# Two-layer network over 16 sequences: the last two blocks as a pair, first-pass steps moved between stages, and the second pass's upper queries in halves

## The reference

```python
# first layer ("first pass")
s = causal_attention(xn)        # 16 heads of 64, softmax over 256 keys, then Wo
g = silu(moe(xn))               # top-1 of 8 experts (352 wide) + a shared expert
# second layer
s = linear_attention(xn)        # 16 heads of 8, elu + 1, cumulative sums
g = silu(transformer(xn))       # two layers l = 0, 1 ("second pass")
# one layer of the transformer: shift tokens, q k v, l2norm, rotary with decay,
# 8 heads of 64, window of 64 tokens:
bk, bv = look_around(bk), look_around(bv)      # the block of 64 before, and its own
mask = (i < j) | (i > j + WINDOW) | (j == -1)  # WINDOW = 64
# then wo, layer norm, glu of width 341, and back to 128
```

## Time and profile before

| | |
|---|---|
| median of 3 runs | 2231.97 us |
| the profiled execution | 2232.22 us, its span 2230.4 us |
| PE busy | 1856.1 us, 83% |
| DVE busy | 1273.5 us, 57% |
| ACT busy | 1248.0 us, 56% |
| POOL busy | 785.9 us, 35% |
| mean granted TensorE clock | 0.914 of full speed |
| chain that ended last | PE 60%, DVE 15%, ACT 9%, issue 8%, POOL 6% |

### The profile page before, as it was taken

How to read it: one execution, slowest core, us unless ns; L and a number is a source line. 1 busy time by engine, 2 the same in 40 slices (tenths; PEclk the granted TensorE clock), 3 DMA queues, 4 the chain that set the end, 5 groups by cost and what they waited for, 6 DMA issues and landing times.

```text
span 2230.4 us, 34655 instructions
## 1 busy us (share of the span) xinstructions
PE 1856.1 (83%) x10900; PEld 1157.0 (52%) x10900; DVE 1273.5 (57%) x4083; ACT 1248.0 (56%) x3559; POOL 785.9 (35%) x912
## 2 busy tenths in 40 slices
PE   6689998997899888987899689987898789858766
PEld 4367764654455455554555345644555445535434
DVE  4434556546755467445754575546745575467654
ACT  2445546754765566656665575656664576346444
POOL 2732225323532343224431353324332343244431
PEclk9889999998999999988999799998999899979878
DMA  8155510000000000000000000000000000000000
GB/s 233 36 173 163 162 39 10 1 1 6 1 1 15 6 1 1 15 1 1 6 6 11 1 1 1 20 1 1 1 13 3 1 1 6 4 2 1 6 0 6
DMA packets 49711, 53.26 MB, mean 24 GB/s; under 512 B 6386, under 2 KB 42236, under 8 KB 49532
## 3 DMA queue, kind: packets, MB, share of 16 engines
q0 software_dynamic: 7808, 27.79, 3.8%
q1 hardware_dynamic: 41724, 23.26, 3.7%
HBM read 41.60 MB, written 9.44 MB: 23 GB/s over the span
## 4 chain that ended last, share of the span: by engine, by line
PE 60%; DVE 15%; ACT 9%; issue 8%; POOL 6%; DMA 1%; DVEq 0%; SPq 0%; POOLq 0%; ACTq 0%
PE ps L552 6%; PE ps L596 5%; PE ps L670 5%; PE ps L568 4%; PE ps L521 4%; PE ps L544 3%; PE ps L541 3%; PE ps L578 3%; PE ps L679 3%; ACT p L813 3%; DVE big L1162 2%; PE ps L512 2%; PE ps L531 2%; POOL h L293 2%; PE ps L725 2%
## 5 line engine op out<-in xcount | busy, mean ns | idle before, releaser
L975 DVE CUSTOM_DVE_ANT_0 p<-ps,mask,nrq 128x128 f32<-128x128 f32 (+1 forms) x512 | 183.0, 413 | 253.4 <-PE ps L544 253.4
L552 PE MATMUL ps<-ident,p 128*128 128x128 f32 x1536 | 250.4, 294 | 48.1 <-ACT p L813 47.3
L1272 POOL COPY rdx<-rden 128x256 f32<-128x256 f32 x256 | 94.7, 399 | 554.6 <-DVE rden L991 554.6
L975 DVE CUSTOM_DVE_ANT_0 p<-ps,mask 128x128 f32<-128x128 f32 (+1 forms) x512 | 152.3, 353 | 232.7 <-PE ps L544 218.1
L552 PEld LDWEIGHTS ps<-ident,p 128*128 128x128 f32 x1536 | 172.8, 147 | 156.6 <-issue 153.1
L813 ACT ACTIVATE p<-p,nmax 128x256 f32<-128x256 f32 x512 | 253.8, 496 | 0.0
L812 ACT ACTIVATE p<-p,nmax 128x128 f32<-128x128 f32 x512 | 200.4, 391 | 67.1 <-DVE nmax L975 66.8
L670 PE MATMUL ps<-wqkv,hT 128*128 128x512 f32 x384 | 208.1, 658 | 27.7 <-ACT big L890 27.3
L826 ACT ACTIVATE pt<-ps 128x384 f32<-128x384 f32 x256 | 125.7, 491 | 175.6 <-PE ps L552 175.6
L531 PE MATMUL ps<-ident,big 128*128 128x128 f32 x512 | 92.2, 325 | 124.7 <-DVE big L1167 94.4
L1377 POOL TENSOR_TENSOR big<-big,rots 128x512 f32<-128x512 f32 x64 | 87.9, 1374 | 274.7 <-ACT big L890 268.2
(11 more groups left out here) (214 smaller groups left out, 3977.6 us busy)
## 6 DMA issues: line engine op xcount, KB each, us to landing
slots_in<-xn SPq DMA_DIRECT2D x1, 2560.0 KB, 14.6
v<-slots_in SPq DMA_DIRECT2D x20, 128.0 KB, 4.7
slots_out<-v SPq DMA_DIRECT2D x20, 128.0 KB, 1.8
big<-in_x SPq DMA_DIRECT2D x4, 512.0 KB, 6.2
x<-in_x SPq DMA_DIRECT2D x8, 256.0 KB, 4.1
out_x<-x SPq DMA_DIRECT2D x8, 256.0 KB, 2.3
wqkv<-in_wqkv SPq DMA_DIRECT2D x2, 768.0 KB
xn<-in_x SPq DMA_DIRECT2D x6, 256.0 KB, 3.2
```

The source lines that it names most:

```text
L552: last = nc.tensor.transpose(bank[:, j * P:(j + 1) * P], c.p[:, u % 4, j * P:(j + 1) * P], c.ident[:, :])
L975: last = V.tensor_tensor_reduce(out=c.p[:, u % 4, a:b], in0=bank[:, a:b], in1=c.mask[st.kind][:, P * (1 - i):SEQ], scale=scale, scalar=3e3 ...
```

## The change

Four things are changed together.

1. **Order.** The prologue leaves ticks 16 to 21, amid the expert stages, without attention; `fill` of the 18 ticks now pauses only at 8, 9, 12 and 13, so that 14 of 18 hold attention (0 to 7, 10, 11, 14 to 17). Each of blocks 0 to 5 so takes 8 first-pass pairs and not 7, and the 64 pairs are used up before block 6. Blocks 6 and 7 then go as a pair: layer 0 of block 6, 2 empty ticks, layer 0 of block 7, 8 empty ticks, layer 1 of block 6, 2 empty ticks, layer 1 of block 7. The side stages go with their blocks. The list has 307 ticks.
2. **Buffers.** Block 7 has its linear attention in buffers that the first pass has left (`attT[0]`, `xnT`, `xn0`); kv, pr and nd of blocks 6 and 7 lie in `v0`. Some waits go, others are added. Counters of the transformer layers follow `plan.turn`, the order in which layers are run.
3. **Logits of the second pass.** The upper queries are taken in two halves of 64 with 128 keys each: 8 matmuls a step where there were 4. The probabilities are 256 columns wide, not 384; the mask, the second exponential, both copies and the transposes (2 a head) shrink with them. Keys 128 to 191 stand in front of 64 to 127 in the first half, so the mask is changed.
4. **Values of the second pass.** 8 matmuls for 4, from 64-row and 128-row pieces, with a wait of PE for the step before and, amid the step, a new semaphore `high_done` of its own.

```diff
+SPANS = [[(0, P), (P, SB)], [(0, P), (P, SEQ)]]
...
+LAST = BLOCKS - 1
...
+        self.layers = [(b, l) for b in range(LAST - 1) for l in range(LAYERS)]
+        self.layers += [(b, l) for l in range(LAYERS) for b in (LAST - 1, LAST)]
+        self.turn = {key: g for g, key in enumerate(self.layers)}
...
-        self.fill(start - 2, ())
+        self.fill(start - 2, range(16, 22))
...
-        for b in range(BLOCKS):
+        for b in range(LAST - 1):
             for i in range(PAIRS):
                 self.steps(1, b, 0, i)
-            self.fill(18, (8, 9, 10, 13, 14, 15))
+            self.fill(18, (8, 9, 12, 13))
             l1 = len(self.ticks)
             for i in range(PAIRS):
                 self.steps(1, b, 1, i)
-            if b + 1 < BLOCKS:
-                lead[b + 1] = l1 - 3
-                self.fill(2, ())
-        self.last = len(self.ticks)
+            lead[b + 1] = l1 - 3
+            self.fill(2, ())
+        assert not self.todo0
+        lead[LAST] = len(self.ticks) - 3
+        for l in range(LAYERS):
+            for i in range(PAIRS):
+                self.steps(1, LAST - 1, l, i)
+            self.ticks += [None] * 2
+            for i in range(PAIRS):
+                self.steps(1, LAST, l, i)
+            if l == 0:
+                self.ticks += [None] * 8
         self.produce = {}
         for key, tick in self.first.items():
             st = self.ticks[tick]
...
-            l0 = self.first[(1, b, 0, 0)]
+            l0 = self.first[(1, b, 0, 0)] + (7 if b == LAST else 0)
...
+    c.xn1 = [sb("xn1", [P, TILES, P])] * LAST + [tiles(c.xnT[:, 0, :])]
...
+    c.qkb = [sb("qkb", [P, TILES, 2 * P])] * LAST + [tiles(spare1[:, 0:2 * TOK])]
...
+    c.v9 = [v9] * LAST + [spare1[:, 2 * TOK:2 * TOK + TILES * LH * LE].rearrange("p (t h e) -> p t h e", t=TILES, h=LH)]
+    c.s1 = [sb("s1", [P, TILES, P])] * LAST + [c.xn0]
...
+    homes = [big] * (LAST - 1) + [spare0] * 2
+    c.kv = [a[:, 0:2 * LH * LD * LE].rearrange("p (t n) -> p t n", t=2) for a in homes]
+    c.pr = [a[:, 2304:3168].rearrange("p (a n) -> p a n", a=2) for a in homes]
+    c.nd = [tiles(a[:, 3168:3744]) for a in homes]
...
+    c.xb = [xb] * LAST + [tiles(c.xnT[:, 1, :])]
...
+def last_keys(plan, mm, g):
+    return mm.full("k", last_pair(plan, 1, *plan.layers[g]))
...
+        if st.kind:
+            m = P + HD
+            for qs, out, ks in ((P, P, P), (P, m, HD)):
+                for h in range(2):
+                    f = HD * h
+                    MM(banks[h][0:HD, out:out + HD], q[f:f + HD, qs:qs + HD], k[f:f + HD, ks:ks + HD], start=True, stop=True)
+            for h in range(2):
+                f = HD * h
+                MM(banks[h][HD:P, P:SEQ], q[f:f + HD, m:SEQ], k[f:f + HD, P:SEQ], start=True, stop=True).then_inc(c.s_full, 1)
+            return
...
-            for j in range(3):
+            for j in range(3 - st.kind):
...
+        v = c.v1[:, plan.turn[(st.b, st.part)] % 2, :, :] if st.kind else c.v0[:, st.part, :, :]
...
+            m, lo, hi = P + HD, slice(0, HD), slice(HD, P)
+
+            def product(keys, t, at, end, **flags):
+                for h in range(2):
+                    f, a = HD * h, st.i * P + HD * h
+                    last = MM(bank[f:f + HD, q + at:q + end], v[keys, 2 * st.s + t, a:a + HD], pts[h][keys, at:end], **flags)
+                return last
+
+            pe.wait_ge(c.pv_done, st.n)
+            product(hi, 0, P, m, start=True, stop=False).then_inc(c.high_done, 1)
+            product(slice(0, P), 0, 0, P, start=False, stop=False)
+            product(slice(0, P), 1, m, SEQ, start=False, stop=False)
+            c.highs += 1
+            pe.wait_ge(c.high_done, c.highs)
+            last = product(lo, 1, P, m, start=False, stop=True)
+            last.then_inc(c.pv_done, 1)
+            return
         for h in range(2):
             f, a = HD * h, st.i * P + HD * h
...
+            end = SPANS[st.kind][1][1]
             A(p[:, 0:P], p[:, 0:P], ACT.Exp, bias=c.nmax[:, u % 4, 0:1], scale=-1.0, accum_out=den[:, 0:1])
-            A(p[:, P:SB], p[:, P:SB], ACT.Exp, bias=c.nmax[:, u % 4, 1:2], scale=-1.0, accum_out=den[:, 1:2])\
+            A(p[:, P:end], p[:, P:end], ACT.Exp, bias=c.nmax[:, u % 4, 1:2], scale=-1.0, accum_out=den[:, 1:2])\
                 .then_inc(c.exp_done, 1)
...
-            for i, (a, b) in enumerate(((0, P), (P, SB))):
+            for i, (a, b) in enumerate(SPANS[st.kind]):
+                mask = c.mask[1][:, a:b] if st.kind else c.mask[0][:, P * (1 - i):SEQ]
                 g = 2 * st.s + i
-                scale = c.nrq[:, st.part, g, 2 * st.i + h:2 * st.i + h + 1] if st.kind else -0.125
-                last = V.tensor_tensor_reduce(out=c.p[:, u % 4, a:b], in0=bank[:, a:b], in1=c.mask[st.kind][:, P * (1 - i):SEQ],
+                scale = c.nrq[:, turn % 2, g, 2 * st.i + h:2 * st.i + h + 1] if st.kind else -0.125
+                last = V.tensor_tensor_reduce(out=c.p[:, u % 4, a:b], in0=bank[:, a:b], in1=mask,
                                               scale=scale, scalar=3e38, op0=ALU.add, op1=ALU.min,
...
+        if 0 < b < LAST:
             pool.wait_ge(c.s_done, s.done("wo", 1, b - 1, 0, 0))
+        elif b == LAST:
...
+        if t == 0 and b < LAST - 1:
+            pool.wait_ge(c.rot_ready, TILES * (plan.turn[(b, 0)] + 1))
+        elif t == 0 and b == LAST:
...
-    before = np.where(i + P <= j + HD, 0, far).astype(np.float32)
-    out["c_mask1"] = np.concatenate([before, near], 1)
+    turned = np.where(np.where(j < HD, j <= i, i <= j - HD), 0, far).astype(np.float32)
+    out["c_mask1"] = np.concatenate([near, np.where(i < HD, turned, near)], 1)
```

More of the change, by code:

```diff
@@ L839, in cum @@
             act.wait_ge(c.sum_ready, u - 1)
-        A(c.pr[:, u % 2, 0:n], bank[:, 0:n], ACT.Copy).then_inc(c.mm_done, 1)
+        A(c.pr[b][:, u % 2, 0:n], bank[:, 0:n], ACT.Copy).then_inc(c.mm_done, 1)
     def xnT(b):
@@ L966, in masked @@
     def masked(st):
+        turn = plan.turn[(st.b, st.part)] if st.kind else 0
         for h in range(2):
```

128 lines of the change are left out of this document (64 added, 64 removed).

## The result

The changed kernel takes 2201.85 us (median of four runs, 2199.92 to 2202.68), against 2231.89 us for the kernel before on the same chip: a ratio of 0.9865, 95% interval 0.9848 to 0.9882. That is 30 us faster (26 to 34 by the interval), where 44 were forecast. The profiled execution of after has a span of 2200.9 us at a granted clock of 0.915.

A forecast was written before the change was run, and what follows sets the result against it. The prediction took the kernel as bound by PE where there is attention and by a chain of latencies in the gaps. Its terms, -9 + 27 - 4 - 58 = -44, gave 2188 us, range 2140 to 2230.

The forecast's parts named there:

- The prologue: Expert ticks without attention: 14 us less, against +5 for work displaced to ticks 40 to 48; sum -9 us (-15 to +3).
- The extra pair: One more pair in the gap of blocks 0 to 5: +4.5 us a block, six times, +27 us (0 to +65).
- the whole price is that of two more steps: Gap of blocks 0 to 5: only two more steps in ticks 14 and 15, and the moved pair, cost time; +4.5 a block.
- dear pair: Rival: the new pair in the gap costs what the others did, six times 9.8 us, 2220 us; chance 0.18.
- blocks of 250 us: Sign of a wrong forecast, in blocks 0 to 5, where 239 + 4 us each was expected.
- The q still waits for rot: Sign of a right forecast: layer 1's first q is still behind a wait for rot; 7.52 us of PE standing still before.
- The steps: Second pass's steps: PE +0.10 us, ACT -0.3 us a step; over 128 steps -4 us (-38 to +36).
- The rival named this: Second-pass steps gain on all engines, 2154 us; halves of logits side by side save another 0.1 us a step; chance 0.13.
- The slower rival: Second pass: the two heads' 64x64 matmuls no longer run beside each other, 0.64 us a step, +82, 2270 us; chance 0.08.
- From tick 253 on: From there to the end, summed piece by piece from nearest stretches: 399.6 us for 457.5, -58 us (-80 to -30).
- The -30: Low-gain bound from tick 253 on: dense ticks and POOL in the empty ones cost 28 us more than the -58.

The follow-up runs named there:

- no_pause: The changed kernel without its six empty ticks among the experts, block 5's gap having 8 of 18 ticks with attention: 2235.49 us, ratio 1.0029.
- one_shape: The changed kernel with the two 64-key value products using all 128 keys, so all value matmuls have one tile shape (result wrong): 2172.06 us, ratio 0.9730.
- halves_after: As halves_first, but both 64-key value products come behind the second part of the logits: 2183.25 us, ratio 0.9782.
- halves_late_qk: halves_first with q or k of a coming pair put behind the step's logits on PE: 2157.09 us, ratio 0.9662.
- halves_first: The changed kernel with 64-key value products moved between the logits' parts two ticks on, for 96 of 128 steps: 2180.51 us, ratio 0.9768.
- fill_q: The changed kernel with seven extra 512-column matmuls on PE ahead of each layer's first q's wait for rot: 2212.19 us, ratio 0.9915.
- pair_in_gap: The kernel before with only the fill changed, 14 of 18 ticks of each gap with attention, old order, buffers and steps: 2257.84 us, ratio 1.0124.
- order_old_steps: The changed kernel with the second pass's steps as before (192 and 384 keys wide, three transposes a head): 2206.98 us, ratio 0.9901.
- no_pause_late_shared: no_pause with the shared expert of blocks 3 to 6 ten ticks later, in layer 1: 2211.28 us, ratio 0.9907.

## Why the prediction was right or wrong

**The prologue: -27 for -9.** The core was right: ticks 15 to 22 take 48.8 us for 63.0, 14.2 less, where 14 were worked out. Two things were missing. The value matmuls of block 1 were counted where they arrive, in the pause, but not where they leave: tick 14 took 11.3 us before and takes 6.7. And the 12 us of displaced PE work were charged to ticks 40 to 48, where they cost 1.0; ticks 22 to 39, which they left, are 8.0 shorter. A good part of it (a wo, the last third of the ffn and down0 of the second block) had moved on into block 0, 15.7 us longer (237.9 for 222.2) where blocks 1 to 4 are 7.6 longer on average. By that comparison about 8 of the 18 us by which this term was too small belong to the next one. It is an estimate: without the pause block 0 takes 235.9 us (no_pause), but with its own shared expert in the gap, so the two effects aren't told apart. By no_pause the pause is worth 25.5 us up to tick 47 and its three pairs cost 21.4 in the gap of block 5: 4 us. The rest of its worth, 27 us, is that it moves the shared expert out of the gap, which the forecast didn't see, and which decides: without it the changed kernel is at 2235.

**The extra pair: +38 for +27.** The step that failed is "the whole price is that of two more steps". With eight pairs in a block for seven, an eighth more of the first pass's other work comes into each block as well: eight value matmuls (twice 3.70 us), two wo (3.81 each) and the shared expert, at least 15 / 8 = 1.9 us of PE. With it the forecast's 4.5 is 6.4, and blocks 1 to 4 measure 7.6 with the shared expert in layer 1, 14 with it in the gap.

The trace of before had this to see. Its block 3 has no shared expert, and one v and one wo for two; here are block 2, with its shared expert in layer 1 as in after, and block 3:

```profile
864.40:1109.40 245.00, 210.55 (x1207) 127.19 (x1206) 145.09 (x462) 145.10 (x413) 88.44 (x100) 0.92 0.02 5
1109.40:1342.10 232.70, 196.96 (x1125) 118.11 (x1124) 136.86 (x451) 139.81 (x404) 78.76 (x92) 0.90 0.02 4
```

Block 3 is 11.7 us shorter than the mean of blocks 1, 2 and 4, 244.4. Of the 7.6 us, that mean leaves 4.7 for the pair, near the forecast's 4.5, and 11.7 / 4 = 2.9 for the work that block 3 lacked. So the size given to the pair itself was about right, and what came with it was at nothing. The stretch of block 5 up to tick 253, also counted at +4.5, is 8.2 us shorter (176.6 for 184.8): before had a shared expert in it, after has not. And block 5 takes seven first-pass pairs in after, not eight. The 38 us are 15.7 for block 0, 30.6 for blocks 1 to 4 and -8.2 for block 5. The rival "dear pair" (10.8 us; its sum of 2220 us is worked out with 9.8, and with 10.8 it would be 2226) named a price that lies between the 7.6 and the 14, without the reason. One sign of being wrong that the prediction gave, blocks of 250 us, has come: 249.2. The q still waits for rot, as was said: 73.4 us of PE's idle time ahead of the transposes of q and k (L555) end with DVE's rot.

```profile
L555 PE MATMUL ps<-ident,big 128*128 128x128 f32 x512 | 86.1, 307 | 111.6 <-DVE big L1225 73.4
```

**The steps: -8 to -12 for -4.** ACT's part was right: its upper exponentials (L866) take 389 ns in the second pass for 496. On PE the three terms were: logits +0.1, values +0.2 net, transposes -0.21. The values came out at 1.006, as worked out (0.80 + 0.28 - 0.11 = 0.97). The logits failed: the halves run at the same time, and L541 to L552, forecast at about 1.0 us, took 0.815. The rival named this, priced it at 0.1 us a step where it was worth 0.19, and had a chance of 0.13 together with the gains on the other engines; by the Trainium skill, TensorEngine Tiling, Available Configurations, 64x64 gives four independent tiles, and the trace agrees with its 0.02 us between the starts of L571 and L574. The cost of a change of shape was taken at 0.14, and one_shape's 0.289 for two confirms it; the same page's Key Properties, that switching the mode drains the engine, is borne out by the 30 us of one_shape, and the 22 us from reordering agree, though part of these may come from the place of the work, as halves_after suggests. The slower rival, heads that no longer run side by side, did not occur.

**From tick 253 on: -40 for -58.** The pieces (us), forecast and measured:

| ticks | forecast | after |
|---|---|---|
| 253 to 260 | 49.7 | 53.0 |
| 260 to 263 | 17.4 | 25.0 |
| 263 to 270 | 64.1 | 55.1 |
| 270 to 273 | 20 | 24.2 |
| 273 to 280 | 41.4 | 42.5 |
| 280 to 289 | 53 | 59.4 |
| 289 to 296 | 59 | 48.3 |
| 296 to 299 | 19 | 26.4 |
| 299 to 306 | 32 | 37.5 |
| 306 to the end | 44 | 45.8 |

The two dense stretches, where the pair of blocks overlaps, were priced 20 us too high: the blocks fit better than feared. The three places without attention that wait for kn were priced 19 us too low, all from one bare row of 17.4 us. In the new order DVE and POOL have the other block's work there. Waits of PE in ticks 260 to 263 and 296 to 299, then POOL in the first of them, then DVE ahead of the second (idle time before, and what ended it, in brackets):

```profile
1856.15 1.09 PE L530 MATMUL ps<-ident,xnT 128*128 128x128 f32 x4 [5.24 <-POOL xnT L306]
2104.61 1.09 PE L555 MATMUL ps<-ident,big 128*128 128x128 f32 x4 [10.07 <-DVE big L1225]
```

```profile
1852.56 0.21 POOL L1407 MEMSET attT<- 128x64 f32 x1 [2.32 <-DVEq L1173]
1852.88 3.13 POOL L306 TENSOR_SCALAR xnT<-x,mv,rstd 128x128 f32<-128x128 f32 x4
```

```profile
2092.48 2.17 DVE L1225 TENSOR_TENSOR big<-big 128x1024 f32<-128x1024 f32 x1
2094.58 0.20 DVE L1202 TENSOR_SCALAR scratch<-v 128x64 f32<-128x64 f32 x1
2094.82 0.55 DVE L1203 RECIPROCAL scratch<-scratch 128x64 f32<-128x64 f32 x1
2095.40 0.90 DVE L1206 TENSOR_TENSOR mn<-v,scratch 128x128 f32<-128x128 f32 x4
...
2103.24 1.22 DVE L1225 TENSOR_TENSOR big<-big 128x1024 f32<-128x1024 f32 x1
```

In ticks 260 to 263 PE stands 5.2 us for the xT of block 7, whose chain is DVE's ln1, a memset of 0.21 us and POOL's ln1n of 3.13: the forecast let the memset and POOL cost nothing "unless POOL comes into the chain", and it did. In ticks 296 to 299 the last rot comes behind o1 of block 7 (1.7 us), four masks and an rr; before, that hole was 3.23 us, and now it is 10.07. Ticks 280 to 289, with 59.4 for 53, are the same kind: POOL is busy for 32.3 us of them. The -30 that the forecast gave as the bound for "dense ticks and POOL in the empty ones" had the second half right. The five pieces left over are 18 us above the forecast together, most in ticks 280 to 289 (6.4) and 299 to 306 (5.5); the second was not looked into.

**The sum.** The three terms missed by +18, -14 and -19 us (in gain). That the total is off by only 14 is luck: a gain too small by 18 stood against two that were too large by 33 together, and inside the last term stretches priced 20 too high stood against 19 and 18 too low. The range held and the sign was right, but the place of the shared expert, worth 27 us, was in no term and no rival.

## What to carry over

Count the changes of TensorE's tile shape along a step before cutting matmuls into smaller ones, and order the pieces so that pieces of one shape stand together: here two of the three further changes a step cost 30 us, and a new order of the same pieces gave 45 us on top of the change (halves_late_qk, 2157 us, is faster than both kernels), of which some may come from shorter queues and not from shapes. When pairs of one loop are moved, list what else of that loop moves with them and where in the other loop's period it lands; the same shared expert cost 6.3 us in layer 1 and 10.7 in the gap. An average over blocks hides what one block lacks: compare blocks with the same work. A wait without cover must be priced with the work that the new neighbours queue on the engines of its chain, not from the bare row.

## What the runs showed of the hardware

- A change of tile shape cost 0.145 us at full clock in the values (two of them 0.289); with 256 of them gone the kernel was 30 us faster, so most of that cost was in the time.
- Matmuls of two kinds of work, logits and values, with 64x64 tiles start 0.02 us apart and run side by side.
- A wait of PE for a semaphore that its own last matmul raises, with nothing between, cost 0.24 us at full clock in the records (1.324 us for 1.083), 96 times. In the time only 2.7 us of it were left (halves_after against halves_first), less than the intervals can tell.
- A higher granted clock is not time: 0.947 to 0.951 for 0.915 to 0.919 came with 10 us more (fill_q against after), though with 112 matmuls added.
- DVE's L1225 of 128x1024 ran 64 times in the trace of after. The 26 times that POOL's L1440 ran beside it, it took 2.17 to 2.19 us, the other 38 times 1.22 to 1.36; L1440 took 2.24 to 2.26 us in those 26 and 1.25 to 1.28 otherwise. So each was about 1 us longer. Beside POOL's L1439 alone (15 times) L1225 stayed at 1.22 to 1.36. By the Trainium skill, GPSIMD Engine Reference, Specifications, the two engines share their interfaces to SBUF and contend where an operation of DVE has two inputs there, as this one has; the rows beside L1440 agree, no run separates it. The last of a layer's four, for which the first q waits, never had L1440 beside it.
- Where every block has the same work, its length mostly repeats, in several kernels to 0.1 or 0.2 us: 256.0 in blocks 1 to 4 of no_pause and pair_in_gap, 249.0 to 249.3 in blocks 3 and 4 of after, order_old_steps and fill_q, 245.7 to 246.0 in blocks 1 to 4 of one_shape, though their steps differ. In these the granted clock also falls at nearly the same places of each block: in no_pause 30.4, 98.7, 132.9, 170.4, 184.0 and 242.1 us after its start, four times over. It isn't a rule: no_pause_late_shared takes 246.8 to 252.4 us for blocks of the same work, and there the clock falls at other places from block to block. That a block's length and the clock hold each other, so that a small gain can vanish in one block and come as several us in another, is what these rows suggest; why stays open.
